# Dealing the work beside the attention scores out anew over a batch's eight steps

## The chip, the cores and the metric

The kernel runs on one core of a Trainium2 chip. The metric is device time in microseconds (us) of one execution. The core has TensorE (PE; its weight loads are shown apart as PEld), VectorE (DVE), ScalarE (ACT), GpSimd (POOL) and SyncE (SP, which here only issues DMAs).

## The reference: what is computed

The input is 8 sequences of 256 tokens with 128 features, in float32. Two transformer layers follow each other. In each layer there is attention with 16 heads of 8 features, then a feed-forward part (FFN), and after each of the two a residual sum and a layer norm.

```
x = layernorm(x + L0_attn(x))     # 16 heads, full softmax over 256 keys
x = layernorm(x + L0_ffn(x))      # 128 -> 512 (dense, then butterfly), exact gelu, butterfly, 512 -> 128
x = layernorm(x + L1_attn(x))     # low-rank q and kv, rotary, 4 shared k/v heads, causal softmax
x = layernorm(x + L1_ffn(x))      # silu(x Wg) * (x Wu) @ Wd with 384 hidden features, int weights / 127
```

The kernel folds the butterflies into dense 128x512 and 512x128 matrices once, on the chip, at the start.

## The kernel before

**Batches and steps.** One sequence in one layer is called a batch here. There are 16: batches 0 to 7 are layer 0, batches 8 to 15 are layer 1. A batch has 16 heads, which are numbered through as m = 0 to 255. Every engine's program is one loop over g (`for g in STEPS`, g rises by 2), and each value of g is one step, which does two heads. So a batch has eight steps, called here by g modulo 16: step 0, 2, ... 14. Within a step PE first does the scores and then whatever other work the table at the top of the file gives to this step.

**Scores.** `max_scores` (L283) computes the scores of heads g+14 and g+15 with queries on the partitions, into one of three PSUM banks SM; DVE takes each row's negated maximum from it into `mx` (L652 in layer 0; L660 with the causal mask in layer 1). `exp_scores` (L302) computes the scores of heads g and g+1 again with keys on the partitions and the maximum subtracted through one more contraction row, into one of three banks ST; ACT takes the exponential into E (L526). Before head 0, PE runs fillers (L313) in the place of L302. Since SM has three banks, PE's max product of a head waits until DVE has reduced the head three before it; the same holds for ST and ACT.

**Work beside the scores.** The table gives for each piece its distance in g from the batch's first head (g = 16 b). The pieces that this text names:

- MT (L339, `AT_MT`): the maxima of eight heads are transposed; ACT copies them to `mt` (L533), and SP sends them by DMA into the extra row of QK (L245). `exp_scores` of those heads waits for that DMA.
- PV (L470, `AT_PV`): E times V for eight heads, 16 small products; ACT copies the result to O (L588). In layer 1 it waits for POOL's causal masking of E (L796).
- T (L346) transposes O; DVE divides by the sums (L668, L671). ATT (L396) transposes again, ACT copies. PROJ (L406) is the output projection; DVE adds the residual and takes statistics (L727, L623, L626).
- LN (`AT_LN`): POOL normalises (L748 to L752) and writes the residual `xb` (L819 or L822). XT (L413, `AT_XT`) transposes the result, ACT copies it to `xt` (L550).
- UP0 (L356, four products c0 to c3 of 512 columns) is the first FFN product of layer 0, once for two batches; DVE adds the bias (L681). GELU (L593, `AT_GELU`) is one ACT instruction over 2048 elements per partition, with an activation table load before it and another behind it. DN0 (L380, two halves of eight products) is the second FFN product; DVE adds and takes statistics (L704). LN0 is POOL's norm of 512 tokens (the same lines L748 to L752, and L829), XT0 (L419) transposes its result and ACT copies (L553).
- UP1 (L367, c0 to c2) and DN1 (L389) are the FFN of layer 1, with ACT's tanh (L540) and DVE's two products (L692, L694); LN1 is its norm and the store.
- QK (L438) and V (L452) make the queries, keys and values of a later batch. SP spreads q and k over the partitions by DMA (L230, `AT_QKIN`). In layer 1 SP first swaps halves (L241) and POOL applies the rotation (L804 to L806, `AT_ROPE`).

**Banks.** All the pieces on PE write to two PSUM banks G in turn: `claim` makes each piece wait until the reader of the piece two before it is done. In one step the pieces come in the order of the program's text: MT, T, UP0, UP1, DN0, DN1, ATT, PROJ, XT, XT0, QK, V, PV. ACT does a step's two exponentials first and then its side work, in nearly that order, GELU last. DVE does a step's two maxima first. POOL's order in a step is mask, rotation, LN, LN0, LN1. Every engine works strictly in its program's order.

**Start.** The loop begins at g = FIRST with the product QK of batch 0. The weights of later stages are sent for by SP one per step from g = LATE = -20 on (L248). POOL folds the butterflies (`paths`, `mix`); the pieces BXU, BXD, TURN, JOIN and BV on PE and ACT belong to this.

## Time and profile before

| | |
|---|---|
| runs before | 402.66, 406.7, 408.13 us; median 406.7 |
| the profiled execution | 402.57 us, its span 400.8 us |
| PE busy | 357.8 us (89% of the span) |
| PE weight loads | 245.6 us (61%) |
| DVE busy | 238.6 us (60%) |
| ACT busy | 204.9 us (51%) |
| POOL busy | 176.2 us (44%) |
| mean granted PE clock | 0.962 of full |

The profile is one execution. Busy shares are unions over the whole span; matmul ends are modelled, so a busy PE isn't PE at its peak. The chain of work that ended last is, by engine, PE 68%, POOL 10%, DVE 8%, issue 6%, ACT 5%. A row of the timeline gives the start, the busy time, engine, line, operation, operands and count; in brackets stands how long the engine sat idle before it and what released it.

### The profile page before, as it was taken

Reading aid. Unit: us, or ns where it says so; the run is one execution under the profiler, and the core shown is the slowest. Engines: PE = TensorE matmul, PEld = TensorE weight load, DVE = VectorE, ACT = ScalarE, POOL = GpSimd, SP = SyncE. Lnnn points to the kernel's source line nnn. Section 1 sums busy time; section 2 is a strip of 40 time slices with the busy share of each in tenths; the row PEclk is TensorE's granted clock in tenths of the full one; section 3 lists DMA queues with packets and bytes.
Section 4 is the critical chain, followed back from the end, with each engine's and each line's share of the span. In section 5 each row is a group of like instructions: output and inputs, shape, how many; then the busy total and the mean of one; then the engine's idle time right before and its main releaser. Section 6 shows DMA issues by size and latency. Waiting matters only on the chain.

```text
span 400.8 us, 10496 instructions
## 1 busy us (share of the span) xinstructions
PE 357.8 (89%) x3912; PEld 245.6 (61%) x3912; DVE 238.6 (60%) x903; ACT 204.9 (51%) x439; POOL 176.2 (44%) x298
## 2 busy tenths in 40 slices
PE   4965999999989999899998979799899999999862
PEld 2543666665657656566557746578577767677541
DVE  3442557567747576375755738476577787863342
ACT  2012666665685456655575535834555565555310
POOL 7035963020201506046142765518776765373541
PEclk9995999999999999899998989989999999999988
DMA  4393132010100101111110111101112120000000
GB/s 148 45 257 63 35 90 78 5 29 3 29 1 9 23 2 42 15 29 28 24 34 2 27 30 29 28 3 34 35 30 42 29 42 2 17 2 16 16 13 13
DMA packets 9218, 14.04 MB, mean 35 GB/s; under 512 B 2000, under 2 KB 4944, under 8 KB 9040
## 3 DMA queue, kind: packets, MB, share of 16 engines
q1 hardware_dynamic: 8656, 13.11, 14.5%
q8 instruction: 31, 0.51, 0.5%
q10 hardware_dynamic: 512, 0.26, 0.4%
q14 instruction: 19, 0.16, 0.1%
HBM read 5.76 MB, written 1.05 MB: 17 GB/s over the span
## 4 chain that ended last, share of the span: by engine, by line
PE 68%; POOL 10%; DVE 8%; issue 6%; ACT 5%; DMA 2%; SPq 1%; POOLq 0%; DVEq 0%; ACTq 0%
PE SM L283 22%; PE G L470 11%; PE ST L302 6%; PE G L367 5%; PE G L380 4%; PE G L356 3%; PE G L438 3%; PE G L406 2%; PE G L389 2%; PE G L346 2%; DMA QK<-mt 2%; POOL ln_f L752 2%; POOL QK L787 2%; PE G L339 2%; DVE gated L692 2%
## 5 line engine op out<-in xcount | busy, mean ns | idle before, releaser
L526 ACT ACTIVATE E<-ST 128x512 f32<-128x512 f32 (+1 forms) x256 | 125.4, 541 | 97.0 <-PE ST L302 96.8
L302 PE MATMUL ST<-QK 32*128 32x256 f32 (+1 forms) x1024 | 138.6, 380 | 14.2 <-DMA QK<-mt 7.2
L283 PE MATMUL SM<-QK 31*128 31x256 f32 (+1 forms) x1024 | 148.7, 381 | 1.2 <-DVE mx L652 1.0
L283 PEld LDWEIGHTS SM<-QK 31*128 31x128 f32 x1024 | 98.9, 186 | 40.5 <-issue 20.1
L652 DVE TENSOR_REDUCE mx<-SM 128x2 f32<-128x512 f32 x128 | 82.5, 687 | 67.7 <-PE SM L283 67.7
L302 PEld LDWEIGHTS ST<-QK 32*128 32x128 f32 x1024 | 93.1, 187 | 18.4 <-ACT E L526 8.9
L660 DVE CUSTOM_DVE_ANT_0 masked_s<-SM,mask_sb 128x256 f32<-128x256 f32 (+1 forms) x256 | 76.0, 353 | 42.5 <-PE SM L283 42.0
L796 POOL TENSOR_SCALAR_AFFINE_SELECT E<-E 128x512 f32<-128x512 f32 x64 | 39.2, 638 | 51.2 <-ACT E L526 51.2
L748 POOL TENSOR_SCALAR nm_a<-mv_a 128x2 f32<-128x2 f32 x16 | 3.1, 193 | 125.2 <-DVE mv_a L626 125.2
L470 PE MATMUL G<-E,V 128*32 128x256 f32 (+1 forms) x1024 | 55.6, 358 | 1.8 <-DVE hid L694 1.1
L470 PEld LDWEIGHTS G<-E,V 128*32 128x32 f32 x1024 | 29.7, 110 | 23.4 <-issue 7.3
L367 PE MATMUL G<-xt,wf 128*128 128x256 f32 x96 | 27.9, 420 | 1.6 <-ACT xt L550 1.5
L588 ACT ACTIVATE O<-G 128x256 f32<-128x256 f32 x32 | 12.2, 381 | 23.2 <-PE G L470 23.2
L660 DVE DVE_READ_ACCUMULATOR2_ANT mx<- 128x1 f32 x256 | 21.2, 83 | 0.0
L367 PEld LDWEIGHTS G<-xt,wf 128*128 128x128 f32 x96 | 17.5, 202 | 5.9 <-issue 1.9
L380 PE MATMUL G<-down,hid 128*128 128x128 f32 x128 | 19.6, 317 | 0.0
L380 PEld LDWEIGHTS G<-down,hid 128*128 128x128 f32 x128 | 18.4, 229 | 1.5 <-issue 0.7
L692 DVE SCALAR_TENSOR_TENSOR gated<-th,G 128x256 f32<-128x256 f32 x24 | 10.1, 422 | 13.6 <-ACT th L540 13.6
L356 PE MATMUL G<-xt,wup 128*128 128x512 f32 x32 | 17.6, 632 | 0.0
L540 ACT ACTIVATE th<-G 128x256 f32<-128x256 f32 x24 | 9.2, 384 | 13.7 <-PE G L367 13.1
L562 ACT ACTIVATE qk<-G,bqk_sb 128x256 f32<-128x256 f32 x16 | 6.7, 471 | 17.2 <-PE G L438 17.2
L752 POOL TENSOR_SCALAR ln_a<-r_a,nm_a,rstd_a 128x128 f32<-128x128 f32 x32 | 14.2, 452 | 1.8
(107 smaller groups left out, 439.0 us busy)
## 6 DMA issues: line engine op xcount, KB each, us to landing
QK<-qk SPq DMA_DIRECT2D x62, 64.0 KB
rs<-ry SPq DMA_DIRECT2D x16, 128.0 KB, 2.3
xb<-x_nat SPq DMA_DIRECT2D x1, 1024.0 KB, 11.5
out<-ln_g SPq DMA_DIRECT2D x8, 128.0 KB, 2.0
xt<-x_t SPq DMA_DIRECT2D x1, 896.0 KB, 6.6
wi<-wi_all SPq DMA_DIRECT2D x1, 576.0 KB, 4.0
QK<-mt SPq DMA_DIRECT2D x32, 8.0 KB
fac<-fac_u SPq DMA_DIRECT2D x1, 508.0 KB, 4.9
```

The costliest lines, as they stand in the source:

```text
L283: ins = nc.tensor.matmul(SM[m % S_RING][:, cols], q, QK[rows, b % QK_RING, r, 1, keys], start=True, stop=True)
L302: ins = nc.tensor.matmul(ST[m % S_RING][:, c * T:(c + 1) * T - q0], QK[rows, b % QK_RING, r, 1, c * P:(c + 1) * P], QK[rows, b % QK_RING, ...
L356: nc.tensor.matmul(bank[:, :], wup[:, c * P:(c + 1) * P], xt[:, n * FT:(n + 1) * FT], start=True, stop=True).then_inc(F0["up_ps"], 1)
L367: ins = nc.tensor.matmul(bank[:, s * T:(s + 1) * T], wf[:, s, c * P:(c + 1) * P], xt[:, i * T:(i + 1) * T], start=True, stop=True)
L380: ins = nc.tensor.matmul(bank[:, i * W:(i + 1) * W], hid0[:, c, s * P:(s + 1) * P], down[:, c, :], start=(c == 0), stop=(c == HC - 1))
L470: ins = nc.tensor.matmul(bank[VCOL * j:VCOL * (j + 1), q0:T], values, E[:, (2 * n + e) % E_RING, j, k * T:(k + 1) * T - q0], start=(e == 0 ...
L526: act.activation(E[:, a % E_RING, j, 0:n], ST[m % S_RING][:, 0:n], ACT.Exp, scale=SCALE)\
L652: ins = nc.vector.tensor_reduce(mx[:, n % 2, :, i], bank[:, :].rearrange("p (q k) -> p q k", q=QT), AX.X, ALU.max, negate=True)
L660: ins = nc.vector.tensor_tensor_reduce(out=masked_s[:, m % 2, lo:hi], in0=bank[:, lo:hi], in1=mask_sb[:, T + lo - hi:T], scale=-1.0, scala ...
L692: link(nc.vector.scalar_tensor_tensor(out=gated[:, i % 2, :], in0=th[:, i % 2, :], scalar=1.0, in1=bank[:, 0:T], op0=ALU.add, op1=ALU.mult))
L752: ins = nc.gpsimd.tensor_scalar(N["ln"][:, parity, s, :], N["r"][:, s, :], N["nm"][:, s:s + 1], N["rstd"][:, s:s + 1], ALU.add, ALU.mult)
L796: nc.gpsimd.affine_select(out=e, in_=e, pattern=[[0, 4], [1, P]], compare_op=ALU.is_ge, fill=0.0, base=0, channel_multiplier=-1).then_inc( ...
```

## The change

The change edits only the table of distances. In layer 0 and 1 alike, values' products (PV) move from distance (10, 18) to (12, 20), that is from steps 10 and 2, which they shared with MT, to steps 12 and 4, where nothing else is. The other pieces move as follows, by step within a batch: QK 8 to 14; V 12 to 0; T 4 to 6; ATT 6 to 8; PROJ 8 to 10; LN 10 to 12; XT 14 to 0 (of the next batch but one); UP1 0, 4, 6 to 2, 6, 8; DN1 12 to 14; UP0 c0 to c2 0, 4, 6 to 2, 6, 8, and c3 12 to 2 (so that c3 comes a batch later); GELU 0 to 2; DN0 4, 12 to 6, 8; LN0 14 to 10. LN1 and XT0 keep their steps, and so does MT. The rotation moves from 12 to 4, the DMA of q and k from 10 (layer 0) and 0 (layer 1) to 0 and 8. Of the pieces that run once, BXD, TURN, JOIN, XB_AT and WF_AT come 4 to 6 later.

```diff
--- before.py
+++ after.py
@@ -41,14 +41,14 @@
 
 
 LEAD = 14
-AT_QK, AT_QKIN, AT_ROPE = -40, (-38, -32), -36
-AT_MT, AT_V, AT_PV = (-6, 2), -4, (10, 18)
-AT_T, AT_ATT, AT_PROJ, AT_LN, AT_XT = 20, 22, 24, 26, 30
-AT_UP1, AT_DN1, AT_LN1 = (32, 36, 38), 44, 50
-
-AT_UP0, AT_GELU, AT_DN0, AT_LN0, AT_XT0 = (48, 52, 54, 60), 64, (68, 76), 78, 80
-
-BXU, BXD, TURN, JOIN, BV, XB_AT, WF_AT, LATE = (4, 6), 12, 28, 16, 0, 10, 34, -20
+AT_QK, AT_QKIN, AT_ROPE = -34, (-32, -24), -28
+AT_MT, AT_V, AT_PV = (-6, 2), 0, (12, 20)
+AT_T, AT_ATT, AT_PROJ, AT_LN, AT_XT = 22, 24, 26, 28, 32
+AT_UP1, AT_DN1, AT_LN1 = (34, 38, 40), 46, 50
+
+AT_UP0, AT_GELU, AT_DN0, AT_LN0, AT_XT0 = (50, 54, 56, 66), 66, (70, 72), 74, 80
+
+BXU, BXD, TURN, JOIN, BV, XB_AT, WF_AT, LATE = (4, 6), 16, 32, 22, 0, 14, 38, -20
 FIRST, FINAL = AT_QK, HEADS + 40
 STEPS = range(FIRST, FINAL, 2)
```

The first place is PE in batch 4, steps 0 and 2 (the GELU of the first two batches is here). SM and ST are the score products, `G<-id,mx` is MT, `G<-E,V` is PV. Before, step 2's scores and what follows:

```order
L283 MATMUL SM<-QK 128x256 x2
L302 MATMUL ST<-QK 128x256 x2
L283 MATMUL SM<-QK 128x256 x2
L302 MATMUL ST<-QK 128x256 x2
L339 MATMUL G<-id,mx 8x128 x2
L470 MATMUL G<-E,V 32x256 x16
L283 MATMUL SM<-QK 128x256 x2
L302 MATMUL ST<-QK 128x256 x2
```

The same place now, from the second half of step 2's scores on:

```order
L283 MATMUL SM<-QK 128x256 x2
L302 MATMUL ST<-QK 128x256 x2
L339 MATMUL G<-id,mx 8x128 x2
L356 MATMUL G<-xt,wup 128x512
L283 MATMUL SM<-QK 128x256 x2
L302 MATMUL ST<-QK 128x256 x2
L283 MATMUL SM<-QK 128x256 x2
L302 MATMUL ST<-QK 128x256 x2
L470 MATMUL G<-E,V 32x256 x16
```

MT is now followed by UP0 c3 (`G<-xt,wup`) and PV stands alone behind the next step's scores.

The second place is ACT around the GELU of batch 4 (`hid<-hid`; `xt`, `mt` and `O` are the copies of XT, MT and PV). Before:

```order
L526 ACTIVATE E<-ST 128x512 [waits a_pv_ps,a_st_ps] x2
L550 ACTIVATE xt<-G 128x256 [waits a_xt_ps]
L526 ACTIVATE E<-ST 128x512 [waits a_pv_ps,a_st_ps] x2
L593 ACT_TABLE_LOAD
L593 ACTIVATE hid<-hid 128x2048 [waits f0_pre_ready]
L526 ACT_TABLE_LOAD [waits a_pv_ps]
L526 ACTIVATE E<-ST 128x512 [waits a_st_ps]
L526 ACTIVATE E<-ST 128x512 [waits a_pv_ps,a_st_ps]
L533 ACTIVATE mt<-G 8x256 [waits m_in3,a_mt_ps]
L588 ACTIVATE O<-G 128x256 [waits a_t_ps,a_pv_ps]
```

Now:

```order
L526 ACTIVATE E<-ST 128x512 [waits a_pv_ps,a_st_ps] x2
L533 ACTIVATE mt<-G 8x256 [waits m_in3,a_mt_ps]
L593 ACT_TABLE_LOAD
L593 ACTIVATE hid<-hid 128x2048 [waits f0_pre_ready]
L526 ACT_TABLE_LOAD [waits a_pv_ps]
L526 ACTIVATE E<-ST 128x512 [waits a_st_ps]
L526 ACTIVATE E<-ST 128x512 [waits a_pv_ps,a_st_ps]
L588 ACTIVATE O<-G 128x256 [waits a_t_ps,a_pv_ps]
L526 ACTIVATE E<-ST 128x512 [waits a_pv_ps,a_st_ps] x4
```

GELU comes one step later, behind the copy of the maxima; its wait for the four biased products (`f0_pre_ready`) stands on the GELU itself, and the table load ahead of it carries no wait.

The third place is POOL in batch 8, around the norm of four row tiles that follows the layer 0 FFN (LN0; `E<-E` is the mask, `ry`, `rs`, `qk` the rotation, `nm_a` begins a batch's LN). Before:

```order
L796 AFFINE_SELECT E<-E 128x4x128 [waits a_exp_done]
L796 AFFINE_SELECT E<-E 128x4x128
L804 TENSOR_TENSOR ry<-ry,ropec_sb 128x512 [waits qk_in1,swapped1]
L805 TENSOR_TENSOR rs<-rs,ropes_sb 128x512
L806 TENSOR_TENSOR qk<-ry,rs 128x512 [waits pool_chain]
L748 TENSOR_SCALAR nm_f<-mv_f 128x4 [waits f0_xt_ps,f0_var_ready]
L749 TENSOR_SCALAR ve_f<-mv_f 128x4
L750 TENSOR_TENSOR rstd_f<-ve_f,half 128x4 [waits pool_chain]
L752 TENSOR_SCALAR ln_f<-r_f,nm_f,rstd_f 128x128 [waits pool_chain]
L752 TENSOR_SCALAR ln_f<-r_f,nm_f,rstd_f 128x128 x3
L829 TENSOR_TENSOR xb<-ln_f,bout_sb 128x512 [waits f0_ln_ready]
L796 AFFINE_SELECT E<-E 128x4x128 [waits a_exp_done]
```

Now:

```order
L796 AFFINE_SELECT E<-E 128x4x128 [waits a_exp_done]
L796 AFFINE_SELECT E<-E 128x4x128
L748 TENSOR_SCALAR nm_f<-mv_f 128x4 [waits f0_xt_ps,f0_var_ready]
L749 TENSOR_SCALAR ve_f<-mv_f 128x4
L750 TENSOR_TENSOR rstd_f<-ve_f,half 128x4 [waits pool_chain]
L752 TENSOR_SCALAR ln_f<-r_f,nm_f,rstd_f 128x128 [waits pool_chain]
L752 TENSOR_SCALAR ln_f<-r_f,nm_f,rstd_f 128x128 x3
L829 TENSOR_TENSOR xb<-ln_f,bout_sb 128x512 [waits f0_ln_ready]
L796 AFFINE_SELECT E<-E 128x4x128 [waits a_exp_done]
L796 AFFINE_SELECT E<-E 128x4x128
L748 TENSOR_SCALAR nm_a<-mv_a 128x2 [waits a_xt_ps,a_var_ready]
L749 TENSOR_SCALAR ve_a<-mv_a 128x2
```

Before, LN0 stood behind the batch's LN, a mask and the rotation, and right ahead of its transposes XT0; now it stands behind one mask only, and the LN of the batch stands behind it and the next mask.

## Rows read from the trace of the kernel before

**Rows 1.** Windows: start:end, length, busy (count) by engine, PEclk, DMA share, GB/s.
```profile
73.68:92.39 18.71, 18.44 (x217) 11.92 (x215) 12.00 (x24) 11.61 (x26) 2.71 (x6) 1.00 0.08 17
73.68:75.25 1.57, 1.57 (x16) 0.98 (x14) 1.08 (x3) 1.08 (x3) 0.00 (x0) 1.00 0.00 0
113.03:158.94 45.91, 43.87 (x477) 28.07 (x476) 28.99 (x61) 28.14 (x53) 13.64 (x23) 1.00 0.07 14
158.94:205.97 47.03, 45.01 (x477) 29.09 (x476) 28.41 (x103) 28.07 (x53) 17.30 (x26) 0.96 0.12 25
205.97:252.78 46.81, 42.17 (x478) 29.53 (x475) 27.63 (x157) 24.60 (x53) 24.37 (x40) 0.93 0.13 25
252.78:301.56 48.78, 44.14 (x517) 33.88 (x517) 31.84 (x175) 26.79 (x59) 28.89 (x48) 0.97 0.13 27
301.56:357.53 55.97, 54.43 (x713) 40.95 (x713) 43.83 (x247) 31.57 (x80) 32.20 (x63) 1.00 0.12 24
```

**Rows 2.** Timeline of PE in batch 3, steps 10 to 14: start, busy, what.
```profile
105.13 0.38 PE L339 MATMUL G<-id,mx 128*8 128x128 f32 x2
105.44 1.93 PE L470 MATMUL G<-E,V 128*32 128x256 f32 x32
107.31 0.48 PE L283 MATMUL SM<-QK 31*128 31x256 f32 x2
...
108.38 1.12 PE L356 MATMUL G<-xt,wup 128*128 128x512 f32 x2
109.35 0.61 PE L452 MATMUL G<-wv_sb,xt 128*128 128x128 f32 x4
...
110.96 0.44 PE L413 MATMUL G<-id,ln_a 128*128 128x128 f32 x2
```

**Rows 3.** Timeline of PE in batch 8, steps 10 and 12.
```profile
222.33 1.51 PE L470 MATMUL G<-E,V 128*32 128x256 f32 x32
223.77 0.48 PE L283 MATMUL SM<-QK 31*128 31x256 f32 x2
...
224.63 2.05 PE L380 MATMUL G<-down,hid 128*128 128x128 f32 x16
226.52 0.61 PE L452 MATMUL G<-wl,xt 128*128 128x128 f32 x4
```

**Rows 4.** Timeline of all engines, around the GELU of batch 4.
```profile
114.14 1.28 ACT L593 ACT_TABLE_LOAD   x1
...
117.36 1.28 ACT L526 ACT_TABLE_LOAD   x1
...
119.30 0.48 PE L302 MATMUL ST<-QK 32*128 32x256 f32 x1 [1.68 <-ACT E L526]
```

**Rows 5.** The same view in batch 3: readers of UP0 and XT.
```profile
109.68 0.74 DVE L681 TENSOR_SCALAR hid<-G,bhid 128x512 f32<-128x512 f32 x1
...
112.10 0.39 ACT L550 ACTIVATE xt<-G 128x256 f32<-128x256 f32 x1
```

**Rows 6.** Timeline of POOL in batches 8 and 9.
```profile
221.98 0.19 POOL L748 TENSOR_SCALAR nm_a<-mv_a 128x2 f32<-128x2 f32 x1 [1.95 <-DVE mv_a L626]
...
223.33 0.89 POOL L752 TENSOR_SCALAR ln_a<-r_a,nm_a,rstd_a 128x128 f32<-128x128 f32 x2
...
229.99 0.20 POOL L748 TENSOR_SCALAR nm_f<-mv_f 128x4 f32<-128x4 f32 x1
...
234.72 1.22 POOL L796 TENSOR_SCALAR_AFFINE_SELECT E<-E 128x512 f32<-128x512 f32 x2
```

**Rows 7.** Timeline of PE at the start of batch 9.
```profile
233.56 0.69 PE L419 MATMUL G<-id,ln_f 128*128 128x128 f32 x4 [2.76 <-POOL ln_f L752]
```

**Rows 8.** Timeline of SP and PE around head 0.
```profile
24.94 0.49 SPq L248 DMA_DIRECT2D fac<-fac_d  x1
25.47 0.57 SPq L245 DMA_DIRECT2D QK<-mt  x1
...
34.16 0.80 PE L302 MATMUL ST<-QK 32*128 32x256 f32 x2 [7.21 <-DMA QK<-mt]
```

**Rows 9.** Windows, as rows 1, around that wait.
```profile
26.00:41.00 15.00, 7.54 (x51) 4.50 (x52) 4.07 (x8) 2.46 (x6) 8.60 (x13) 0.66 0.53 94
```

## The prediction

> **What bounds the kernel now.** I read the page first (PE has the largest busy share), then the chain of waits, then the table of windows, one for each batch or pair of batches between its first exponentials, and last the timeline inside a step. The windows say where time is lost [rows 1], the timeline what a piece of work costs PE when nothing is in its way [rows 2, 3]: the distance from one piece's start to the next one's. Read so, with layer 0 first: a step's scores 1.07 (107.31 to 108.38), in layer 1 0.86 (223.77 to 224.63); MT 0.31; PV 1.87 (105.44 to 107.31), in layer 1 1.44; UP0 0.97 (108.38 to 109.35); DN0 1.89 a half (224.63 to 226.52). Estimates from these: QK and UP1 have as many columns as UP0, 0.97; V and PROJ 0.53; XT and ATT 0.37; T 0.5, XT0 0.6; DN1 has 12 of DN0's 16 products, 1.42.
>
> Add up the pieces of a stretch and compare with its length [rows 1]. Batch 2: 8 x 1.07, 2 x 1.87, 2 x 0.31, T 0.5, ATT and XT 0.7, V and PROJ 1.1, QK 1.0 are 16.2 of 18.7, 2.5 lost. Batches 4 and 5: 16 x 1.07, 4 PV, 4 MT, 2 QK and 4 UP0, 2 DN0, and the small ones (5.2) are 40.6 of 45.9, 5.3 lost. Batches 6 and 7: again 40.6 of 47.0, 6.4 lost. Batches 8 and 9: 36.0 of 46.8, 10.8 lost. Batches 10 and 11 (UP1 and DN1 come in): 40.4 of 48.8, 8.4 lost. Batches 12 to 14: 52.0 of 56.0, 4.0 lost. So PE's work bounds the kernel, and what a new table can win is only what is lost. It has four sources:
>
> - **Light steps.** The step with nothing beside its scores lasts 1.57, not 1.07 [rows 1]: with three banks PE waits for DVE's maxima. Steps 0, 6 and 14 are such steps or hold one small transpose, while steps 2 and 10 hold MT and PV, 3.25 in all.
> - **The GELU stops.** ACT goes from 114.14 to 118.64 with table load, GELU and table load [rows 4] and takes no exponentials; PE covers this with a step's scores, MT and PV, then sits idle 1.68 (the half-done score block makes it about 2.1). There are four such stops.
> - **The clock.** The granted clock is 1.00 in batches 4 and 5, but 0.96, 0.93 and 0.97 in the next three pairs, 1.9, 3.3 and 1.5 us of clock time. The stretches at 1.2 instead of 2.4 GHz come right behind idle time of PE of about 2 us or more, each worth some 1.7 us.
> - **XT0.** LN0 stands on POOL behind LN, mask and rotation, and PE waits 2.76 for it in batch 9 [rows 7].
>
> **The change part by part.** No instruction is added or removed.
>
> *Light steps.* Now each step holds something: V and XT in 0, MT and a piece of UP in 2, PV alone in 4 and 12, and so on to QK in 14. In batches 0 to 2, without FFN, MT (1.38 by pieces) and ATT (1.44) still stand alone, and MT takes the empty step's floor of 1.57, ATT what it lacks for DVE's turn, about 0.5; I leave 1.0 of the 2.5: 3 x 1.5 = **-4.5**. In batches 12 to 14 no step is below 1.7 by pieces; DVE is busy 43.8 of 56.0 there [rows 1], so its work still comes in lumps (T, UP1 and PROJ in steps 6 to 10, as in 4 to 8 before). I leave 1.5 of 4.0: **-2.5**.
>
> *PV alone.* A step's scores and PV are 2.94 in layer 0, where MT and PV took 3.25: nothing is won by itself, MT's 0.31 goes along. MT is now followed by a full-width product instead of PV. Its 0.31 may become 0.2 less or 0.4 more, 26 times at most; the nearest rows, those of a narrow piece between others [rows 2], give 0.31, and I take no difference. The Trainium skill, in TensorEngine Tiling (Array Packing), Key Properties, says that changing the tiling mode, unlike changing the tile, drains the engine; MT (8 columns) and PV (32 columns) may share a mode that UP0 and PROJ don't. By it the sum would lose the larger of these bounds; no row before shows MT with a full-width successor, so it is left to the range.
>
> *The GELU stops.* GELU moves to step 2, into the same step as its last input, UP0 c3. The bias sum ends 2.04 behind UP0's start (108.38 to 110.42) [rows 2, 5], so counting from the start of step 2's scores it ends at 1.07 + 0.31 + 2.04 = 3.4. The table load is not behind that wait in ACT's order and is over at 3.9; GELU, table load and one exponential let PE go on at 7.7. PE has covered until 1.38 + 0.97 + 1.07 + 1.87 + 0.3 = 5.6: a stop of 2.1, as before. Would the table load wait, it would be 3.0. In batch 10 UP1 c0 and its tanh come in between, 2.9. I take 2.1, 2.1, 2.0 and 2.9, and half-clock stretches behind the last three as now, and behind the first with chance one half.
>
> *XT0 and XT.* LN0 now has three steps before XT0, so the 2.76 goes. But the batch's own LN now stands behind it. LN0 takes 4.7 (229.99 to 234.72), a mask 1.2, LN until its product 2.2 (221.98 to 224.22) [rows 6]: 8.2 behind the end of DN0's statistics. In layer 0 PE has as much work until XT (10 to 14, and the scores of 0). In batch 8 steps are shorter, and I count 12.3 on POOL against 9.9 on PE from the start of step 8: a new wait of 2.5 at XT, at the head of batch 9; in batch 11, where UP1 and DN1 fill PE, 1.0.
>
> *Three pieces in step 0.* In odd batches step 0 has XT, XT0 and V; V claims XT's bank, and ACT copies XT only after two exponentials: XT ends at 111.4 and is copied at 112.49 [rows 2, 5]. V waits 0.7 to 0.8 in batches 5 and 7.
>
> *Together by stretch* (lost before, lost after, difference; small rest 0.6 in each pair). Batches 4 and 5: 5.3; 2.1 + 0.8 clock + 0.8 V + 0.6 = 4.3; **-1.0**. 6 and 7: 6.4; 2.1 + 1.7 + 0.8 + 0.6 = 5.2; **-1.2**. 8 and 9: 10.8; 2.0 + 1.7 + 2.5 + 0.8 (half a chance of a slow stretch behind XT) + 0.6 = 7.6; **-3.2**. 10 and 11: 8.4; 2.9 + 1.7 + 1.0 + 0.8 (DN0 behind T's bank) + 0.8 = 7.2; **-1.2**. UP0 c3 leaves batch 3 and comes back in batch 10, no difference.
>
> *Start.* Head 0 waits 7.21 for the DMA of the maxima, issued at 25.47 behind a queue of loads and landed near 34.1 [rows 8]. SP's order now has batch 2's q and k (four DMAs of 64 KB) behind it, and two 64 KB weights earlier. About 400 KB of some 3 MB that went out in 16 us lie no longer ahead: 2.2 by share, 0 if the last big load alone decides; I take **-1.6**. V of batch 0 stood ahead of this wait, hidden; now it is behind it, at the half clock: **+0.9**.
>
> *End.* DN1 of batch 13 and XT of batch 14 fall behind the last scores, 1.8 of PE, and the last batch gets shorter by 0.5 to 1: **+0.8**. The chain from the last PV on is the same.
>
> SP's queue gets q and k of layer 1 at step 8, behind the rotation at step 4: five steps, over 10 us, before their first use, against 2.7 of issue; the DMAs of the maxima go out at 4 and 12 as before. On POOL the rotation delays mask 8, which PV at 12 needs, by some 4 us of 8. I cost both at nothing.
>
> Sum: -4.5 - 2.5 - 1.0 - 1.2 - 3.2 - 1.2 - 1.6 + 0.9 + 0.8 = **-13.5**. Against the profiled execution's 402.57 this gives 389.1. The median of the runs, 406.7, is 4.1 above that execution; with this on top it is 393.2. I take 391, between the two.
>
> **Rivals.**
> - *As worked out*, 387 to 396: 0.57.
> - *The new waits lower the clock too.* Rows for: in the pairs from batch 6 on, clock was lost behind GELU stops and the XT0 wait [rows 1]. Against: batches 2, 4 and 5 have many short waits and a clock of 1.00. If V's four waits and batch 4's stop each bring 1.7, 8.5 comes back: 397.6, with the runs' 4.1 401.7, no change. The Trainium skill, in TensorE: Matmul & The Clock Gate, A second HAM failure mode, tells of a kernel whose PE idles briefly between groups so often that its clock swings; the 1.00 of batches 2, 4 and 5 speaks against it here. 0.18.
> - *Gains larger*: no slow stretch at all any more (6.7 back), or the queue at the start empties 2.5 earlier: 382 to 386. 0.11.
> - *Light steps don't give back*, since DVE's lumps and ACT's copies set the pace: half of 7.0, 395 to 398. 0.08.
> - *Slower.* PE's clock after long stops. Behind the 7.21 wait at the start the clock is 0.66 over 15 us [rows 9], 5.1 lost, where a GELU stop of 2.1 loses 1.7. If stops of 2.5 to 3 us (table load behind the wait, XT of batches 9 and 11) already cost like the long one, six stops lose 3.4 more each, and 2.9 comes from the loads: 389.1 + 20.4 + 2.9 = 412.4, 416.5 on the runs' scale. It decides from a stop somewhere between 2.1 and 7.2. 0.06.
>
> That the change doesn't part MT and PV is excluded by the order of PE.
>
> **Numbers.** 391 is the likeliest. The range takes in the larger gain and most of the clock case, and the bounds of the table load (2.9) and MT: 382 to 402. A measurement tells about 2% from no change here, which is 398.6 and 414.8. Faster: 0.57 + 0.11, and a part of the two next cases, 0.74; slower 0.06; the rest, 0.20, within.
>
> **What would show it.** Batches 0 to 2 at 17.2 each and 12 to 14 at 17.5 to 18 between first exponentials, with no step under 1.57; PE idle behind GELU 1.7 to 2.9 four times, not longer; no wait of L419 for POOL, but one of L413 of 1 to 2.5 in batches 9 and 11; table load ahead of GELU ending before the bias sum; the DMA of the first maxima landing at 32 to 33; a mean clock of 0.96 or 0.97. A clock under 0.95, or a wait of PV (L470) for POOL or for ACT's exponentials, would make it wrong.

## The result and the profile after

The changed kernel took 382.6 us, the median of four runs (380.35 to 383.52), against 404.69 for four runs of the kernel before on the same chip (402.66 to 408.13). The ratio is 0.944, with an interval of 0.935 to 0.953: faster by 5.6%. The forecast was 391, in a range of 382 to 402. The direction was right; the gain of some 22 us was 1.6 times the 13.5 of the sum, and the result stands at the range's edge. A ratio leaves out runs over 1.5% above the fastest of the same kernel, while a median takes in all, and the profiles of experiments 5, 10, 13 and 15 are of such slower runs.

The profiled execution took 382.55 us with a span of 380.8, against 402.57 and 400.8 before. First the page: busy time of PE, the granted clock in 40 slices, the chain of work that ended last.

```profile
PE 344.2 (90%) x3912; PEld 240.1 (63%) x3912; DVE 237.0 (62%) x903; ACT 204.2 (54%) x439; POOL 176.1 (46%) x298
PEclk9996999999999999999998989879999999999988
PE 78%; POOL 7%; DVE 5%; ACT 4%; issue 3%; DMA 2%; POOLq 0%; DVEq 0%; ACTq 0%
```

The work is the same and PE's share of the chain rose from 68% to 78%. The windows that answer to [rows 1], for batch 2, batches 4 and 5, 6 and 7, 8 and 9, 10 and 11, and 12 to 14 (start:end, length, busy time of PE, PEld, DVE, ACT and POOL, PEclk, DMA share, GB/s):

```profile
67.29:86.13 18.84, 17.96 (x222) 11.62 (x222) 11.88 (x24) 12.12 (x27) 2.71 (x6) 1.00 0.09 17
105.07:148.76 43.69, 41.17 (x478) 26.57 (x478) 28.74 (x61) 27.98 (x54) 9.81 (x20) 1.00 0.07 14
148.76:192.16 43.40, 40.88 (x478) 26.47 (x477) 28.25 (x103) 27.80 (x52) 17.35 (x26) 1.00 0.14 27
192.16:236.10 43.94, 39.57 (x478) 28.98 (x478) 27.42 (x157) 24.72 (x52) 26.23 (x42) 0.92 0.13 26
236.10:285.15 49.05, 44.78 (x520) 34.97 (x520) 32.38 (x176) 26.92 (x59) 28.90 (x50) 0.93 0.13 27
285.15:337.81 52.66, 51.75 (x714) 40.13 (x714) 43.21 (x244) 31.24 (x79) 34.68 (x61) 1.00 0.14 31
```

The whole span cut in the same way, at the first exponential of each stretch. Lengths in us; the differences are against before, as forecast and as measured.

| stretch | before | after | forecast | measured |
|---|---|---|---|---|
| start to the first exponential | 36.26 | 29.71 | -1.6 | **-6.6** |
| batches 0 to 2 (V of batch 0 with them) | 56.13 | 56.42 | **-3.6** | **+0.3** |
| batch 3 | 20.64 | 18.94 | 0 | -1.7 |
| 4 and 5 | 45.91 | 43.69 | -1.0 | -2.2 |
| 6 and 7 | 47.03 | 43.40 | -1.2 | -3.6 |
| 8 and 9 | 46.81 | 43.94 | -3.2 | -2.9 |
| 10 and 11 | 48.78 | 49.05 | -1.2 | +0.3 |
| 12 to 14 | 55.97 | 52.66 | -2.5 | -3.3 |
| batch 15 and the end | 43.27 | 42.96 | +0.8 | -0.3 |
| sum | 400.8 | 380.8 | -13.5 | -20.0 |

The two largest errors pull in opposite directions and nearly cancel: the start gave 5.0 more than forecast (four times its term), the first three batches 3.9 less (nothing). The other 5.4 of the 6.5 between the sums lie in batches 4 to 7 (3.6 more), batch 3 (1.7), the end (1.1) and 12 to 14 (0.8), less the 1.8 by which batches 8 to 11 fell short. The forecast moved UP0 c3 (0.97) from batch 3 to batch 10 without a term in either row; it is 1.0 of batch 3's 1.7 and of the 1.6 by which batch 10 grew (27.33 to 28.94).

The waits of PE in the changed kernel (in all, times, longest):

```profile
PE ST L302 <- ACT E L526: 8.0, 4, 2.6
PE G L413 <- POOL ln_a L752: 6.6, 5, 2.6
PE ST L302 <- DMA QK<-mt: 1.8, 1, 1.8
```

No wait of L419 for POOL is left (2.76 in [rows 7]), the one of L413 that was forecast is there, and the DMA of the maxima is waited for 1.8 instead of 7.2. The four GELU stops are as they were.

**The start in the rows.** SP's DMAs (`SPq`) and PE at head 0, after the change:

```profile
20.81 0.43 SPq L248 DMA_DIRECT2D fac<-fac_d  x1
22.55 0.58 SPq L245 DMA_DIRECT2D QK<-mt  x1
27.06 1.32 SPq L230 DMA_DIRECT2D QK<-qk  x2
28.55 0.48 PE L302 MATMUL ST<-QK 32*128 32x256 f32 x2 [1.76 <-DMA QK<-mt]
```

The spread of batch 2's q and k now leaves behind the maxima instead of ahead of them. The maxima leave 2.9 earlier (22.55 against 25.47) and are 6.0 under way instead of 8.7. That is 5.6; the other 0.9 is the clock, since head 0's products no longer run at half speed: 0.48 against 0.80 in [rows 8]. How far the price by bytes was off can be read from the kernel before, in windows of its wait:

```profile
22.00:26.00 4.00, 3.91 (x40) 2.62 (x38) 2.96 (x5) 0.76 (x2) 0.80 (x3) 1.00 0.99 379
28.00:30.00 2.00, 0.00 (x0) 0.00 (x0) 0.00 (x0) 0.00 (x0) 0.64 (x1) 0.80 1.08 117
30.00:32.00 2.00, 0.00 (x0) 0.00 (x0) 0.00 (x0) 0.00 (x0) 0.00 (x0) 0.50 1.04 98
```

All DMA engines are busy in each of the three, but they move 379 GB/s in the first and about 100 in the last two. In these two the spread and the load of `fac_d` (508 KB, issued right behind it) share the engines: the packets of 4064 bytes, which are the load's, make up 142 of the 197 KB that start in the third window, and take 0.58 us each, where such packets took 0.16 to 0.18 from 21.5 to 23. So this is not the rate of the spread alone. In the changed kernel it has the engines nearly to itself, and they are then less than half busy:

```profile
28.00:30.00 2.00, 1.45 (x15) 1.09 (x16) 0.69 (x2) 0.29 (x1) 0.00 (x0) 1.00 0.43 101
```

SP's own issue of the four DMAs (256 KB in 2.6 us) comes to the same 100 GB/s, so this window doesn't show what limits the spread. The experiments show what its place in the queue costs; why the load beside it slows down stays open.

### The profile page after: what moved, and what is told of

Read it like the earlier page. It is cut to its first block, busy times and chain, and to the rows that moved or that the text cites. A ratio compares the mean times of both kernels' runs of the same rounds, so it can differ in the third digit from the quotient of the medians.

```text
span 380.8 us, 10496 instructions
## 1 busy us (share of the span) xinstructions
PE 344.2 (90%) x3912; PEld 240.1 (63%) x3912; DVE 237.0 (62%) x903; ACT 204.2 (54%) x439; POOL 176.1 (46%) x298
## 4 chain that ended last, share of the span: by engine, by line
PE 78%; POOL 7%; DVE 5%; ACT 4%; issue 3%; DMA 2%; POOLq 0%; DVEq 0%; ACTq 0%
PE SM L283 27%; PE G L470 13%; PE ST L302 5%; PE G L367 5%; PE G L380 5%; PE G L356 4%; PE G L438 3%; PE G L339 3%; PE G L346 3%; PE G L389 2%; PE G L452 2%; POOL QK L787 2%; PE G L406 2%; DMA QK<-mt 2%; PE ST L444 1%
## 5 line engine op out<-in xcount | busy, mean ns | idle before, releaser
L302 PE MATMUL ST<-QK 32*128 32x256 f32 (+1 forms) x1024 | 138.8, 382 | 9.8 <-ACT E L526 8.0
L283 PE MATMUL SM<-QK 31*128 31x256 f32 (+1 forms) x1024 | 141.5, 382 | 0.6 <-DVE mx L652 0.5
L283 PEld LDWEIGHTS SM<-QK 31*128 31x128 f32 x1024 | 94.4, 188 | 40.4 <-DVE mx L652 13.3
L302 PEld LDWEIGHTS ST<-QK 32*128 32x128 f32 x1024 | 92.0, 188 | 14.0 <-ACT E L526 10.0
L748 POOL TENSOR_SCALAR nm_f<-mv_f 128x4 f32<-128x4 f32 x4 | 0.8, 196 | 41.7 <-DVE mv_f L626 41.7
L380 PE MATMUL G<-down,hid 128*128 128x128 f32 x128 | 18.3, 304 | 0.0
L356 PE MATMUL G<-xt,wup 128*128 128x512 f32 x32 | 16.8, 606 | 0.0
L533 ACT ACTIVATE mt<-G 8x256 f32<-8x256 f32 x32 | 11.4, 358 | 7.0 <-PE G L339 7.0
```

The costliest lines, as they stand in the source:

```text
L283: ins = nc.tensor.matmul(SM[m % S_RING][:, cols], q, QK[rows, b % QK_RING, r, 1, keys], start=True, stop=True)
L302: ins = nc.tensor.matmul(ST[m % S_RING][:, c * T:(c + 1) * T - q0], QK[rows, b % QK_RING, r, 1, c * P:(c + 1) * P], QK[rows, b % QK_RING, ...
L356: nc.tensor.matmul(bank[:, :], wup[:, c * P:(c + 1) * P], xt[:, n * FT:(n + 1) * FT], start=True, stop=True).then_inc(F0["up_ps"], 1)
L380: ins = nc.tensor.matmul(bank[:, i * W:(i + 1) * W], hid0[:, c, s * P:(s + 1) * P], down[:, c, :], start=(c == 0), stop=(c == HC - 1))
```

## The experiments

The medians of the kernel before lay between 404.7 and 405.5 on the chips used; a ratio is always against the runs of it on the same chip. A version of the changed kernel differs from it for certain only where its interval lies clear of 0.935 to 0.953.

### The start

**1. Only the spread of batch 2 moved, in the kernel before** (from g = -6 to g = -2, behind the first maxima):

```diff
+SPREAD2 = -2
-                    if (b := batch_at(g, AT_QKIN[l], (l,))) is not None:
+                    b = batch_at(g, AT_QKIN[l], (l,))
+                    if l == 0 and b == 2:
+                        b = None
+                    if l == 0 and g == SPREAD2:
+                        b = 2
+                    if b is not None:
```

> The kernel before, with one thing moved: SP issues the four DMAs that spread batch 2's q and k behind the DMA of the first maxima and not ahead of it. Theory (the spread is slow on the DMA engines, and it stood between head 0 and its maxima): head 0's scores start 4 to 6 us earlier than 34.16, and the time falls by 4 to 6 us against the kernel before. Rival (only bytes count, as the prediction had it): 1 to 2 us. Rival (the early start of the changed kernel comes from the other pieces that moved): under 1 us.

Measured: 401.1 us, ratio 0.991 (0.987 to 0.994). The first exponential is at 32.45 instead of 36.26, 3.8 earlier:

```profile
23.15 0.58 SPq L251 DMA_DIRECT2D QK<-mt  x1
30.35 0.80 PE L308 MATMUL ST<-QK 32*128 32x256 f32 x2 [2.87 <-DMA QK<-mt]
```

The DMA of the maxima leaves 2.3 earlier (23.15 against 25.47), since SP isn't held by issuing the spread, which the forecast had left out altogether; and it is 1.5 less under way. In the profile batch 0 got 1.6 longer, at a clock of 0.82 instead of 0.91, and the spans are only 1.0 apart (399.8 and 400.8); the medians are 3.9 apart. The bytes-only rival is refuted; the theory's 4 to 6 us are just missed.

**2. The changed kernel with batch 2's q and k back ahead of the maxima** (its QK product at g = -8 and the spread at -6; the same edit as in 1 with `SPREAD2 = -6`, and a `qk_at(g)` that gives batch 2 at -8):

> The changed kernel, with batch 2's QK product and the DMAs of its spread put back to g = -8 and -6, where the kernel before has them. Theory (spread ahead of the maxima costs the start): head 0's scores start at 33 to 34 instead of 28.55, the time is 387 to 389, 5 us above the changed kernel. Rival (bytes only): 384. Then the rest of the change, some 16 us, is what the dealing of the steps gives.

Measured: 389.1 us, ratio 0.962 (0.956 to 0.969). The first exponential is at 36.36, and from batch 1 on each step has the length that it has in the changed kernel, to 0.03. Head 0 waits again:

```profile
34.26 0.80 PE L313 MATMUL ST<-QK 32*128 32x256 f32 x2 [7.07 <-DMA QK<-mt]
```

So the start is worth some 6.5 of the change (the clock of batch 0, which lasts 19.57 here, is in it), and all other table entries together some 16 us.

**3. SP's whole order of the change at the start, in the kernel before** (as 1, and two weights of the late list sent for earlier):

```diff
+                if g == AT_QKIN[0] + 4:
+                    for loaded, dst, src in late[:2]:
+                        sp.dma_start(dst, src).then_inc(loaded, 16)
-                if 0 <= (i := (g - LATE) // 2) < len(late):
+                if 2 <= (i := (g - LATE) // 2) < len(late):
```

> The kernel before, with batch 2's spread behind the first maxima as in the run that moved it alone, and besides with the two loads of the projection's weights issued ahead of batch 1's spread, so that SP's order until the first maxima is the changed kernel's. Theory (the whole early start is SP's order: spread and loads): head 0's exponential at 29.5 to 30.5 instead of 36.26, 6 us faster than the kernel before. Rival (the rest of the start comes from PE: the MT of the changed kernel comes earlier because the QK product of batch 2 is behind it): 32 to 33 again, 4 us faster.

Measured: 398.0 us, ratio 0.982 (0.978 to 0.985), 7.0 us, as the theory had it. The first exponential, though, is at 32.5, where the rival had it, for a reason that neither gave. Head 0 doesn't wait for the DMA of the maxima at all:

```profile
31.37 0.48 PE L311 MATMUL ST<-QK 32*128 32x256 f32 x2
```

In this profile PE ran at half clock from 16.08 to 26.32, which costs 5.1 of clock time, and MT starts at 26.80 instead of 21.79. Batch 0 then runs at full clock and lasts 17.1, so that batch 1 begins at 49.6, against 54.6 before and 48.6 after. SP's order thus brings all but 1 us of the early start of batch 1 without a change on PE; where the first exponential would stand with the same clock as before, this one profile doesn't show.

### PV alone, or with MT

**4. The changed kernel with PV back in steps 10 and 2**

```diff
-AT_MT, AT_V, AT_PV = (-6, 2), 0, (12, 20)
+AT_MT, AT_V, AT_PV = (-6, 2), 0, (10, 18)
```

> The changed kernel, with only values' products put back to distances 10 and 18, so that they share steps 10 and 2 with the maxima and steps 12 and 4 hold nothing beside the scores. Theory (a step without side work costs its floor, 1.57 in layer 0 and about 1.3 in layer 1, instead of the 1.07 and 0.86 of its scores): 32 such steps, 0.4 to 0.5 each, 13 to 16 us slower than the changed kernel, 396 to 399. Rival (it doesn't matter where the products stand, the gain is from GELU, norms and start): 382 to 385.

Measured: 418.3 us, ratio 1.034 (1.030 to 1.037): 36 us slower than the changed kernel, and 13 slower than before. No theory expected this much. PE and ACT in batch 3, step 2:

```profile
89.90 1.02 PE L356 MATMUL G<-xt,wup 128*128 128x512 f32 x2
91.22 1.93 PE L470 MATMUL G<-E,V 128*32 128x256 f32 x32 [0.29 <-ACT mt L533]
```

```profile
89.84 1.09 ACT L526 ACTIVATE E<-ST 128x512 f32<-128x512 f32 x2 [0.25 <-PE ST L302]
90.81 0.36 ACT L533 ACTIVATE mt<-G 8x256 f32<-8x256 f32 x1
```

MT, UP0 and PV claim two banks, so PV, the third, needs MT's bank back, and ACT copies MT only after the step's two exponentials. The wait recurs in every batch, and PE's weight loads show it in full:

```profile
PEld G L470 <- ACT mt L533: 19.1, 26, 1.1
```

That explains the waits, 19.1 us at most. The rest is the lumps: a step of 4.49 (3.64 in layer 1) is followed by an empty one of 1.87 (1.61), which PE's 1.07 cannot shorten. And the GELU steps grow from 5.86 + 1.48 + 3.85 to 8.30 + 1.73 + 5.21, because the only long product that covered the stop now stands ahead of GELU (a stretch at half clock, 120.80 to 124.21, lies in the last two of these). The parting of MT and PV is thus what the other entries need: with it undone the same table is slower than before. What the parting would give alone, in the kernel before, was not run.

### The light steps

**5 and 6. Maxima over the first 128 keys only, in both kernels** (layer 0; DVE's instruction falls from 0.687 to 0.421 us). The other half of each row isn't read, so the exponentials have another offset.

```diff
-   bank[:, :].rearrange("p (q k) -> p q k", q=QT),
+   bank[:, :].rearrange("p (q k) -> p q k", q=QT)[:, :, 0:P],
```

In the kernel before:

> The kernel before, with DVE's maxima of layer 0 (L652) taken over the first 128 keys of 256 only (the maxima are those of half the keys). Theory (light steps are held at 1.57 to 1.96 by PE's wait for these maxima): L652 falls from 0.69 to about 0.4 and the light steps of batches 0 to 7 to 1.1 to 1.5, 0.4 each for some 22 of them, 7 to 10 us faster than the kernel before. Rival (the floor is PE's own, or ACT's exponentials at 1.09 a step): under 2 us.

Measured: 403.9 us, ratio 0.991 (0.986 to 0.995), 1 us where 7 to 10 were expected. In the changed kernel:

> The changed kernel with the same halved maxima of layer 0 (over half the keys). Theory (the new table has filled the light steps, so DVE's maxima hold PE up less): 2 to 4 us faster than the changed kernel, 378.5 to 380.5, much less than the same edit gives the kernel before. Rival (the steps with only MT, ATT or MT and PROJ, at 1.87, still wait for DVE): 6 us or more, as much as before.

Measured: 386.0 us, ratio 0.951 (0.947 to 0.955), no faster than the changed kernel's 382.6 (the intervals overlap). The theory that DVE sets the light steps failed for the most part. In the kernel before the empty step goes from 1.57 to 1.48 only, and most steps with one small piece from 1.87 to 1.96 down to 1.64 to 1.69, while step 8 grows from 2.68 to 2.80. In the changed one, in batches 1 and 2, the MT step goes from 1.87 to 1.60 and the ATT step from 1.89 to 1.66, but the PV step behind MT grows from 2.98 to 3.22; from batch 3 on hardly a step changes. Some 0.3 of a filled light step is DVE; near 1.5 there is a floor that DVE's speed doesn't move. PE, ACT and the three banks ST remain for it; which of them sets it was not measured. And in its profile the changed kernel lost more by the clock than it won: batches 4 and 6 took 24.9 each instead of 23.34, with stretches at half clock that weren't there before.

**7. BXD, TURN and JOIN later, in the changed kernel**

```diff
-BXU, BXD, TURN, JOIN, BV, XB_AT, WF_AT, LATE = (4, 6), 16, 32, 22, 0, 14, 38, -20
+BXU, BXD, TURN, JOIN, BV, XB_AT, WF_AT, LATE = (4, 6), 18, 40, 34, 0, 14, 38, -20
```

> The changed kernel with the three pieces that run once in other steps: BXD from step 0 to step 2 of batch 1, JOIN from step 6 of batch 1 to step 2 of batch 2, TURN from step 0 to step 8 of batch 2. Theory (batches 0 to 2 gained nothing because these pieces came into full steps, TURN as a third one): batch 1 falls by 0.7 to 1, batch 2 by 1, 1.5 to 2.5 us faster. Rival (these batches are held by something else): no difference.

Measured: 383.3 us, ratio 0.946 (0.944 to 0.948), the same as the changed kernel. In the changed kernel TURN is a third piece in step 0 of batch 2, behind XT and V:

```profile
67.12 0.44 PE L413 MATMUL G<-id,ln_a 128*128 128x128 f32 x2
67.40 0.61 PE L452 MATMUL G<-wv_sb,xt 128*128 128x128 f32 x4
68.71 0.66 PE L506 MATMUL G<-id,up 128*128 128x128 f32 x4 [0.70 <-ACT xt L550]
```

That step takes 3.25; in experiment 7 and in batch 3, with XT and V alone, it takes 1.89. Batch 1 falls from 18.66 to 18.28 and batch 2 from 18.84 to 18.14 (JOIN now adds 0.3 in its step 2, and TURN 0.3 in step 8 instead of 1.36 in step 0), 1.1 together. The gain is real in the steps and absent in the time: batches 4 and 6 took 24.9 and 26.5 instead of 23.34, again by half clock, while batches 0 and 10 had less of it (17.61 and 27.43 instead of 18.92 and 28.94).

### The GELU stops

**8 and 9. Tanh in the place of GELU, in both kernels**: the same ACT instruction without the two table loads. The function is another one.

```diff
-   act.activation(hid0[:, :, :], hid0[:, :, :], ACT.Gelu)
+   act.activation(hid0[:, :, :], hid0[:, :, :], ACT.Tanh)
```

> The kernel before, with tanh in the place of gelu at L593 (another function, same instruction size, no table load before or behind it). Theory: each of the four stops was 2.1 us and brought a stretch at 1.2 GHz with it in most cases; without 2.57 of table loads PE no longer stops: 11 to 14 us faster than the kernel before, and no slow stretch between 60 and 340 us but that behind XT0's wait. Rival (the stops are short of cost, PE has the work to catch up): under 6 us.

> The changed kernel with the same edit (tanh in the place of gelu). Theory (the change left the GELU stops as they were, 2.1 to 2.9 each, and their clock): 10 to 14 us faster than the changed kernel, 369 to 373, about as much as before. Rival (the change has covered part of the stops): at least 3 us less than the same edit gives the kernel before.

Measured: 390.9 us, ratio 0.964 (0.960 to 0.968), in the kernel before, and 369.6, ratio 0.910 (0.906 to 0.914), in the changed one: 14 and 13 us. The stops cost the same in both within the noise; the change left them alone, as forecast. PE's waits of L302 for ACT are gone from both profiles, and the instruction itself takes 1.91 as before. Between 60 and 340 us each profile has one stretch at half clock left, behind the wait for POOL (2.77 and 2.65) in batch 9. So eight loads of 1.28 us (10.2 us on ACT) cost the kernel 13 to 14 with the clock that they lose.

**10. V at step 4 for batches 4 to 11, in the changed kernel**, a step behind the GELU (the replaced line stands in PE's program and in ACT's):

```diff
+def v_at(g):
+
+    for offset in (AT_V, AT_V + 4):
+        b = batch_at(g, offset)
+        if b is not None and (4 <= b < 12) == (offset != AT_V):
+            return b
+    return None
-                if (b := batch_at(g, AT_V)) is not None:
+                if (b := v_at(g)) is not None:
```

> The changed kernel with the product of the values (V) of batches 4 to 11 at step 4 instead of step 0, ahead of PV. Theory (the GELU stop is ACT's 4.5 us less what PE has to do, so 0.53 more of work behind it comes out of the stop; and step 0 of odd batches loses its third piece): steps 2 to 6 of batches 4, 6, 8 keep their sum while step 0 is at its floor of 1.6 to 1.9, odd batches 0.3 shorter each; 1 to 3 us faster. Rival (V only makes step 4 longer): 0 to 2 us slower.

Measured: 375.2 us, ratio 0.924 (0.920 to 0.928).

```profile
PE ST L311 <- ACT E L535: 5.4, 4, 1.9
```

PE does V between the scores of step 4 and PV, while ACT is at the GELU. The stops fall from 8.0 in all and 2.6 at most to 5.4 and 1.9, but batch 4 as a whole stays as it was (23.36 against 23.34): V fills the stop and costs nothing there, and step 0 was at its floor without it. In batches 5 and 7, 0.55 is won, since V no longer waits behind XT and XT0. That is far less than the 7 us between the medians; the rest goes with the clock. The granted clock of the four runs is 0.968, 0.981, 0.990 and 0.982, where the changed kernel had 0.961 to 0.970. The profile, of the first of these, still has half-clock stretches in batches 6, 8, 9 and 10, the first of them (156.34 to 159.75) behind a stop of only 1.18:

```profile
155.02 0.48 PE L311 MATMUL ST<-QK 32*128 32x256 f32 x1 [1.18 <-ACT E L535]
```

### LN0, XT0 and POOL

**11. The changed kernel with LN0 at its old distance**

```diff
-AT_UP0, AT_GELU, AT_DN0, AT_LN0, AT_XT0 = (50, 54, 56, 66), 66, (70, 72), 74, 80
+AT_UP0, AT_GELU, AT_DN0, AT_LN0, AT_XT0 = (50, 54, 56, 66), 66, (70, 72), 78, 80
```

> The changed kernel, with only the norm of four row tiles (LN0) put back to step 14. Theory (its new place took away the wait of XT0 but brought the wait of XT): L413 waits no more for POOL in batches 9 and 11, L419 waits instead, 2 to 4 us in batch 9; the time is within 2 us of the changed kernel's. Rival (LN0's early place is itself a gain of 3 us or more): 386 or more. Rival (its early place is a loss): 380 or less.

Measured: 386.0 us, ratio 0.951 (0.948 to 0.957), 3.4 above the changed kernel, though the intervals overlap: the theory's 2 us and the rival's 386 are not told apart. L419 waits for POOL again, 7.4 in all. The theory left out batches 5 and 7, where it waits 1.75, with half clock behind it: their step 0 lasts 5.83 and 5.78 instead of 3.30 and 3.23. In batches 9 and 11 nothing is lost on the whole (6.63 against 6.32; 3.42 against 3.73): there one wait stands in the other's place.

**12. LN0 one step later, at 76 instead of 74, in the changed kernel**

> The changed kernel with the norm of four row tiles (LN0) at step 12, behind the batch's own LN in POOL's order and not ahead of it. Theory (the 2.6 wait of XT at the head of batch 9 and its fellow in batch 11 come from LN0's 4.7 us ahead of LN): L413 no longer waits in batches 9 and 11, L419 doesn't either (two steps left before XT0), 2.5 to 4 us faster than the changed kernel, 379 to 380. Rival (LN0 then stands ahead of the mask, and values' products or XT0 wait instead): 382 to 384.

Measured: 383.3 us, ratio 0.944 (0.939 to 0.948): no difference, as the rival had it. The wait of L413 in batch 9 is gone and one of L419 is there (and step 0 of batches 5 and 7 grows to 4.30 and 4.22):

```profile
218.60 1.09 PE L419 MATMUL G<-id,ln_f 128*128 128x128 f32 x4 [2.79 <-POOL ln_f L752]
```

**13. LN0 at 76 and XT0 at 84, so that XT0 comes two steps later as well**

```diff
-AT_UP0, AT_GELU, AT_DN0, AT_LN0, AT_XT0 = (50, 54, 56, 66), 66, (70, 72), 74, 80
+AT_UP0, AT_GELU, AT_DN0, AT_LN0, AT_XT0 = (50, 54, 56, 66), 66, (70, 72), 76, 84
```

> As the one before, and the transposes of LN0's result (XT0) at step 4 instead of step 0. Theory (step 0 of odd batches holds three pieces, and the third waits 0.7 to 0.8 for ACT's copy of the first): step 0 of batches 5 and 7 falls from 3.3 to 1.9, step 4 rises by 0.6, net 0.8 in each of four batches, 2 to 4 us faster than with LN0 at step 12 alone. Rival (the wait only moves to step 4's product): no difference.

Measured: 377.7 us, ratio 0.929 (0.923 to 0.935). Batches 5, 7, 9 and 11 last 19.53, 19.25, 18.42 and 18.64 instead of 20.35, 20.06, 21.17 and 20.11: 5.9 in all, 4.9 in the median. In batch 9 the wait of XT (2.62) goes, with the stretch at half clock that followed it, and a wait of PV for the mask (1.4) comes in step 4.

**14. XT0 at 84 in the kernel before**

> The kernel before, with the transposes of LN0's result (XT0) at step 4, two steps after where they stood. Theory (in the kernel before XT0's wait for POOL costs 2.8 in batch 9, 1.5 in batch 11, 0.6 each in 5 and 7, and a slow stretch): 4 to 6 us faster than the kernel before, no wait of L419. Rival (step 4 has then three pieces, and the third waits for the first one's reader): 1 to 3 us faster.

Measured: 409.6 us, ratio 1.012 (1.008 to 1.017), 1% slower, which neither theory had. POOL and PE in batch 9:

```profile
231.15 0.19 POOL L748 TENSOR_SCALAR nm_f<-mv_f 128x4 f32<-128x4 f32 x1
...
235.85 2.39 POOL L796 TENSOR_SCALAR_AFFINE_SELECT E<-E 128x512 f32<-128x512 f32 x4
```

```profile
237.22 1.13 PE L470 MATMUL G<-E,V 128*32 128x256 f32 x20 [4.08 <-POOL E L796]
```

PE no longer waits for LN0 and runs on to PV at step 2, whose masks stand on POOL behind LN0's 4.7 us. In the changed kernel, where LN0 is earlier and PV a step later, XT0 at the same distance (with LN0 at 76) wins 5.

### Do the gains add?

**15. 13 and 7 together** (the two edits as they stand there)

> The changed kernel with LN0 at step 12, XT0 at step 4 and the three pieces that run once moved (BXD and JOIN to steps 2, TURN to step 8), all three of which were run apart. Theory (the gains are in different steps and add): batches 5, 7, 9 and 11 as short as with the norm's move, batches 1 and 2 as short as with the pieces' move, 1 us under the run with LN0 and XT0 moved, 375 to 377, if the clock's slow stretches stay as many. Rival (a shift of the start moves slow stretches onto more of the stops and eats it): 377 to 380.

Measured: 378.4 us, ratio 0.930 (0.925 to 0.935), as 13 alone. Batch 2 (18.14) and the odd batches (19.53 and 18.40 for 5 and 9) have the lengths found apart, and batch 1 is 0.4 shorter than in 7 (17.87), so in the steps it adds. In its profile batches 4 and 6 took 24.95 each, where in that of 13 only batch 6 did.

**16. 13, and V at step 4 for batches 4, 6, 8 and 10 only**

```diff
+        if b is not None and (b in (4, 6, 8, 10)) == (offset != AT_V):
```

> The changed kernel with LN0 at step 12 and XT0 at step 4, and V at step 4 instead of 0 for batches 4, 6, 8 and 10 alone (those with a GELU), so that the odd batches keep the light step 0. Theory (stops decide): the GELU stop seen by PE gets shorter by V's 0.5 in each even batch, the odd batches keep 19.5, 19.3, 18.4 and 18.6, and shorter stops bring fewer slow stretches: 371 to 375 us. Rival (the clock takes it back): the lengths are the same, but stretches at half clock appear behind the four stops as in the version with LN0, XT0 and the start's pieces: 376 to 380. Second rival: V in step 4 now stands next to PV and XT0 of the other batch and claims wait for ACT's copies: odd batches longer, 378 or more.

Measured: 372.7 us (370.76 to 375.09), ratio 0.919 (0.915 to 0.924), the fastest of all: 10 us under the changed kernel, 33 under the one before. Batches 4 and 5, 6 and 7, 8 and 9, 10 and 11 in its windows:

```profile
105.40:148.29 42.89, 41.70 (x478) 26.83 (x477) 28.82 (x61) 27.76 (x53) 9.81 (x20) 1.00 0.07 15
148.29:190.91 42.62, 41.43 (x477) 26.74 (x477) 28.35 (x103) 27.59 (x52) 17.35 (x26) 1.00 0.14 27
190.91:230.56 39.65, 37.07 (x478) 26.75 (x477) 27.34 (x157) 24.36 (x53) 26.23 (x42) 1.00 0.15 29
230.56:275.86 45.30, 42.69 (x519) 32.70 (x519) 32.38 (x176) 26.54 (x58) 29.19 (x51) 1.00 0.13 29
```

The clock is 1.00 in all four pairs, with stops of at most 1.9, where the changed kernel has 0.92 and 0.93 in the last two. Of the 9.2 us between the two profiled spans, 1.6 is in batches 4 to 7 and 8.0 in batches 8 to 11 (the first stretches are 0.3 longer). What the slow stretches lost there in the changed kernel, 0.08 of 43.94 and 0.07 of 49.05, is 6.9 in clock time.

Against experiment 13 V alone has moved, and it shortens no batch by itself (batch 4: 23.34 there, 23.36 here). The 5 us between the medians are the clock's: batches 6, 8 and 10, with half-clock stretches in the profile of 13, take 23.36, 21.22 and 26.37 instead of 24.95, 22.76 and 28.72. Over runs this repeats: with V behind the GELU (experiments 10 and 16) the granted clock of ten runs is 0.968 to 0.990; with V in step 0 (the changed kernel and 7, 11, 12, 13 and 15) that of 26 runs is 0.953 to 0.981.

## Why the prediction was right in direction and wrong in size

**The step that failed most is *Start*.** It priced the batch 2 spread and the two weights by their bytes ("2.2 by share, 0 if the last big load alone decides; I take -1.6"), with 2.2 as the upper end. Measured is 6.55. Three things were missing: SP's 2.6 us to issue the spread (experiment 1: 2.3 of it came back), a queue that moves some 100 GB/s with all DMA engines busy while spread and load share them, where loads move 379, and the half clock behind the long wait (0.9). The windows over 28 to 32 of the kernel before show the second; the prediction used only the one from 26 to 41 [rows 9], whose mean of 94 GB/s at a share of 0.53 hides it. One part of the rival "Gains larger" was this ("the queue at the start empties 2.5 earlier"), with the right place and under half the size.

**The second is *Light steps* in batches 0 to 2.** Forecast -4.5, and with V +0.9; measured +0.3. The steps themselves did nearly what was said; two things that the forecast set at nothing took the gain. The first is the clock. Batch 0 in the kernel before, in the changed one, and in experiment 11, which has the changed kernel's order there:

```profile
36.26:54.61 18.35, 18.01 (x191) 12.12 (x191) 10.18 (x17) 11.83 (x26) 17.88 (x18) 0.91 0.23 57
```

```profile
29.71:48.63 18.92, 18.85 (x183) 12.68 (x184) 10.31 (x18) 11.25 (x25) 16.89 (x19) 0.82 0.21 40
```

```profile
30.03:46.33 16.30, 16.09 (x183) 10.85 (x184) 10.28 (x18) 11.14 (x25) 14.16 (x15) 1.00 0.23 46
```

At full clock batch 0 takes 16.30. Before, most of the half clock lay within the 7.2 us wait, where it cost nothing; with the wait short it falls into work, 1.8 more in clock time (0.18 of 18.92 less 0.09 of 18.35). Experiment 3 has the order of the kernel before there at full clock, 17.12: at equal clock the new order won 0.8, near the forecast's 1.5 less 0.9 for V. The second is the once-run pieces, which the text of the change moved and the forecast never priced: TURN costs 1.36 in step 0 of batch 2 (3.25 against 1.89), most of the forecast's gain for that batch. Without it batch 2 would be 17.48 where 17.2 was forecast; the last 0.3 is the MT step, 1.87 instead of the 1.57 that the prediction gave it. The reason given for the floor was wrong too: the prediction laid it to DVE's maxima, and with these at 0.421 instead of 0.687 the empty step fell from 1.57 to 1.48 only (experiment 5). In batches 12 to 14, with neither, the same term was good: 3.3 against 2.5.

**The third is the clock of batches 4 to 7**: 2.5 us at half clock were in the forecast (0.8 and 1.7), and the profile has none there, but a second stretch in batch 10. Over batches 4 to 11 the forecast had 6.7 lost and the profile shows 6.9 (0.08 of 43.94 and 0.07 of 49.05), where [rows 1] give 6.6: the places were wrong, and that the sum came out is luck, since the clock's share changes from run to run (0.961 to 0.970 over the four). **The last is the scale**: the 1.9 that was put on top because the median of before stood 4.1 over its profile. The changed kernel's median is its profiled time.

That 382.6 is still inside the range of 382 to 402 is luck as well: the two largest errors, 5.0 us in the start and 3.9 in the first three batches, had opposite signs.

What held:

- *The GELU stops* are still there at their forecast size. The rows that answer to [rows 4]:

```profile
106.81 0.38 PE L339 MATMUL G<-id,mx 128*8 128x128 f32 x2
107.02 1.02 PE L356 MATMUL G<-xt,wup 128*128 128x512 f32 x2
108.09 0.75 DVE L681 TENSOR_SCALAR hid<-G,bhid 128x512 f32<-128x512 f32 x1
108.31 1.28 ACT L593 ACT_TABLE_LOAD   x1
109.61 1.91 ACT L593 ACTIVATE hid<-hid 128x2048 f32<-128x2048 f32 x1
111.53 1.28 ACT L526 ACT_TABLE_LOAD   x1
113.48 0.48 PE L302 MATMUL ST<-QK 32*128 32x256 f32 x1 [1.85 <-ACT E L526]
```

  The table load runs while DVE still adds the bias (108.09 to 108.84), so it didn't wait; the stop is 1.85 where 1.68 was. In batch 10 it is 2.56, forecast 2.9.
- *XT0 and XT.* Forecast was that L413 waits 2.5 in batch 9 where L419 had waited 2.76. POOL stands as counted, LN behind LN0 and a mask:

```profile
209.17 0.20 POOL L748 TENSOR_SCALAR nm_f<-mv_f 128x4 f32<-128x4 f32 x1 [6.13 <-DVE mv_f L626]
...
213.87 1.22 POOL L796 TENSOR_SCALAR_AFFINE_SELECT E<-E 128x512 f32<-128x512 f32 x2
215.07 0.20 POOL L748 TENSOR_SCALAR nm_a<-mv_a 128x2 f32<-128x2 f32 x1
...
216.43 0.88 POOL L752 TENSOR_SCALAR ln_a<-r_a,nm_a,rstd_a 128x128 f32<-128x128 f32 x2
```

```profile
217.45 0.41 PE L413 MATMUL G<-id,ln_a 128*128 128x128 f32 x2 [2.62 <-POOL ln_a L752]
```

- *Three pieces in step 0.* The forecast was 0.7 to 0.8 in batches 5 and 7. V waits 0.47 for ACT's copy there, and taking XT0 out of V's step won 0.8 in each (experiment 13).
- *MT before a full-width product.* In batch 4 MT starts at 106.81 and UP0 at 107.02: 0.21, 0.1 less than the 0.31 that was taken and well inside the bounds (0.2 less, 0.4 more). The Trainium skill's rule in TensorEngine Tiling (Array Packing), Key Properties, by which a change of mode drains the engine, shows no cost here.
- *Slower*, by longer stops that cost like the long one: the stops stayed under 2.7, and a slow stretch still loses 1.6 (24.95 against 23.34). But the rival *The new waits lower the clock too* named a real danger: in the profiles of three versions (experiments 6, 7 and 15) the clock took what the steps had won. These stretches came behind the GELU stops of batches 4 and 6 (1.85), which have the same length in the changed kernel and brought none there; none came behind V's waits of 0.5. The Trainium skill, in TensorE: Matmul & The Clock Gate, A second HAM failure mode, tells of clock swings from many brief idles; batches 4 to 7, with such waits and a clock of 1.00, don't show that.

Still open: which of PE, ACT and the banks sets the floor near 1.5 of a light step; why loads slow down beside the spread; and what decides at which of the four stops the clock falls. The higher clock of experiments 10 and 16 fits shorter stops, but in the profile of 10 a stretch follows a stop of 1.18, and stops of 1.85 often brought none. Stops of fixed length were not tried.
